# Reordering the layer norm's power, the unit maxima, the scatters and one score maximum in a sixteen-image attention pipeline

## What is computed

```python
x = x + _L0_conv_ref(_gn(x), w_qkv, pos_embedding, w_out, b_out)   # group norm, windowed attention
t = _to_tokens(x)                                                  # 16 images x 256 tokens
t = t + _L1_attn_ref(_ln_t(t), w_qkv, b_qkv, w_out, b_out)         # layer norm, full attention per image
t = t + _L1_ffn_ref(_ln_t(t), router_w, ..., fc2_b)                # layer norm, 8 experts, 2 per token
```

```python
dots = jnp.einsum('bhwid,bhwjd->bhwij', q, k) * scale
dots = dots + pos_embedding[_REL_IDX[:, :, 0], _REL_IDX[:, :, 1]]
attn = jax.nn.softmax(dots, axis=-1)
out = jnp.einsum('bhwij,bhwjd->bhwid', attn, v)
```

## Time and profile before

| | us |
|---|---|
| three runs | 706.55, 712.59, 710.5 |
| median | 710.5 |
| the profiled execution, as the device reports it | 709.77 |
| span of that execution in the profile | 708.0 |

### The profile page before, as it was taken

The page is one execution under the profiler, slowest core; times in us unless marked ns, Lnnn a source line. Parts: engine busy times, 40 slices in busy tenths (PEclk is TensorE's granted clock), DMA queues, the critical chain, the costliest instruction groups (busy, mean ns, idle before and its releaser), DMA issues.

```text
span 708.0 us, 18292 instructions
## 1 busy us (share of the span) xinstructions
PE 598.8 (85%) x6460; PEld 479.6 (68%) x6460; DVE 438.5 (62%) x1325; ACT 410.4 (58%) x915; POOL 396.2 (56%) x503
## 2 busy tenths in 40 slices
PE   4877889999989899899899998988975799999910
PEld 3656667777767777677677776766655688888810
DVE  5534666767767677677776777765433365555625
ACT  2445576787676667766767677444411366666600
POOL 5665653454546576665665765642376066666643
PEclk9799999999999999999999999999996899999975
DMA  7100220231422414224133242243841122233237
GB/s 213 25 2 1 54 54 13 50 69 56 120 43 91 118 37 119 57 86 126 42 104 89 66 122 57 85 124 91 270 182 49 47 87 87 84 91 91 72 135 254
DMA packets 54511, 63.08 MB, mean 89 GB/s; under 512 B 12978, under 2 KB 47794, under 8 KB 53906
## 3 DMA queue, kind: packets, MB, share of 16 engines
q1 hardware_dynamic: 48294, 49.59, 25.3%
q0 software_dynamic: 4544, 9.38, 3.9%
q10 hardware_dynamic: 1584, 2.95, 1.2%
HBM read 35.74 MB, written 28.64 MB: 91 GB/s over the span
## 4 chain that ended last, share of the span: by engine, by line
PE 42%; POOL 17%; issue 15%; DVE 10%; ACT 7%; DMA 6%; SPq 2%; ACTq 0%; DVEq 0%; POOLq 0%
POOL slots L549 5%; POOL pa L623 4%; POOL pa L631 3%; PE pG L1192 3%; PE pSA L1264 3%; DMA slots<-sel_dram 2%; PE pSB L1438 2%; PE pTA L1438 2%; PE pTB L1438 2%; PE pSA L1438 2%; PE pTA L1349 2%; DVE pa L994 2%; PE pOA L1449 2%; PE pOB L1449 2%; PE pOB L1293 2%
## 5 line engine op out<-in xcount | busy, mean ns | idle before, releaser
L623 POOL TENSOR_TENSOR pa<-pa,mxa 128x512 f32<-128x512 f32 x64 | 66.7, 1042 | 110.9 <-DVE mxa L1017 110.8
L664 POOL DMA_INDIRECT ysl<-yo,dst x78 | 75.5, 968 | 59.7 <-DVE yo L1154 45.3
L631 POOL TENSOR_TENSOR pa<-pa,rca 128x512 f32<-128x512 f32 x64 | 67.0, 1047 | 63.5 <-DVE rca L1037 63.3
L760 ACT ACTIVATE ptb<-pTB 128x512 f32<-128x512 f32 x128 | 76.6, 599 | 43.1 <-PE pTB L1275 42.7
L549 POOL DMA_INDIRECT slots<-rec,slot x64 | 65.1, 1017 | 15.9 <-issue 13.2
L777 ACT ACTIVATE pta<-pTA 128x512 f32<-128x512 f32 x64 | 38.5, 602 | 56.1 <-PE pTA L1349 55.6
L1027 DVE TENSOR_REDUCE sma<-pa 128x8 f32<-128x512 f32 x64 | 43.8, 684 | 37.8 <-ACT pa L754 37.8
L754 ACT ACTIVATE pa<-pa 128x512 f32<-128x512 f32 x64 | 40.2, 628 | 42.2 <-POOL pa L623 41.9
L1349 PE MATMUL pTA<-ident,pa 128*128 128x128 f32 x256 | 40.3, 281 | 24.0 <-DVE pa L994 14.7
L979 DVE TENSOR_REDUCE mxb<-pSA 128x2 f32<-128x512 f32 x64 | 44.0, 688 | 25.1 <-PE pSA L1240 24.5
L1275 PE MATMUL pTB<-q,kbd 100*128 100x256 f32 x256 | 56.1, 301 | 0.1
(11 more groups left out here) (227 smaller groups left out, 1738.3 us busy)
## 6 DMA issues: line engine op xcount, KB each, us to landing
slots<-sel_dram SPq DMA_DIRECT2D x16, 1040.0 KB
kbd<-kst SPq DMA_DIRECT2D x128, 48.0 KB, 2.2
q<-qst SPq DMA_DIRECT2D x64, 96.0 KB, 2.2
xt<-slots SPq DMA_DIRECT2D x39, 130.0 KB, 2.2
xch<-x_ch_dram SPq DMA_DIRECT2D x4, 512.0 KB, 5.8
xt<-x_tok_dram SPq DMA_DIRECT2D x16, 128.0 KB, 2.3
xch<-t SPq DMA_DIRECT2D x16, 128.0 KB, 4.6
fw<-f_dram SPq DMA_DIRECT2D x1, 2048.0 KB
```

The lines of the kernel that those rows point to most:

```text
L623: pool.tensor_tensor(pa[:, u, :, :], pa[:, u, :, :], mxa[:, u % 2, :].unsqueeze(2).to_broadcast([128, 8, WIN]), ALU.subtract).then_inc(sa_ ...
L631: pool.tensor_tensor(pa[:, u, :, :], pa[:, u, :, :], rca[:, b, :].unsqueeze(2).to_broadcast([128, 8, WIN]), ALU.mult).then_inc(sa_nrm, 1)
L664: pool.indirect_dma_start(ysl, bass.IndirectOffsetOnAxis(ap=dst[:, t % YB, n:n + 1], axis=0), yo[:, t % YB, n, :], None).then_inc(y_dma[t ...
L760: a.activation(ptb[:, h % PTBUFS, :, :], pTB[:, :].rearrange("p (a b) -> p a b", a=2), ACT.Exp).then_inc(st_exp, 1)
```

## The change

The same instructions run, with the same operands and the same waits; six blocks of code stand elsewhere. On DVE the unit maxima of u = 0 and 2 come directly behind the bias adds of steps 0 and 4, and those of u = 1 and 3 directly behind the reciprocals of steps 1 and 5, instead of at steps 2 and 6. At step 6 the score maximum comes ahead of the two remainders. On POOL the power for `tn1` goes from step 4 to step 3, behind `mine` and ahead of L631; the two scatters of step 3 go behind L631; the bias add `t1b` of step 5 goes behind L631. The lists of PE, ACT and SP are the same.

```diff
@@ POOL, iteration
-                    if n == 4 and M is not None:
-                        pool.wait_ge(m_eps, M.j + 1)
-                        pool.tensor_tensor(rs1[:, :], rs1[:, :], half[:, 0:2], ALU.pow).then_inc(m_pow, 1)
-                    if n == 5 and M is not None:
-                        pool.wait_ge(m_t, M.j + 1)
-                        wait(pool, r_t, M.j - TB + 1)
-                        pool.tensor_tensor(t1b[:, M.j % TB, :, :], t1[:, :, :], bo1s[:, :, :], ALU.add).then_inc(m_tb, 1)
...
-                    if n == 3:
-                        depart(K, n)
+                    if n == 3 and M is not None:
+                        pool.wait_ge(m_eps, M.j + 1)
+                        pool.tensor_tensor(rs1[:, :], rs1[:, :], half[:, 0:2], ALU.pow).then_inc(m_pow, 1)
...
-                    if n != 3:
-                        depart(K, n)
+                    if n == 5 and M is not None:
+                        pool.wait_ge(m_t, M.j + 1)
+                        wait(pool, r_t, M.j - TB + 1)
+                        pool.tensor_tensor(t1b[:, M.j % TB, :, :], t1[:, :, :], bo1s[:, :, :], ALU.add).then_inc(m_tb, 1)
+                    depart(K, n)
@@ DVE, iteration
-                    if M is not None and n == 6:
...
-                        v.scalar_tensor_tensor(kst1[:, 1, :], pM[:, 0:TOK], bk1s[:, 0:1], kst1[:, 0, :].bitcast(f32),
...
                         v.tensor_reduce(mxb[:, Bm.par, n % 2, n // 2 * 2:n // 2 * 2 + 2], bank[:, :].rearrange("p (a k) -> p a k", a=2), AX.X,
                                         ALU.max, negate=True).then_inc(sb_max, 1)
+                    if M is not None and n == 6:
...
+                        v.scalar_tensor_tensor(kst1[:, 1, :], pM[:, 0:TOK], bk1s[:, 0:1], kst1[:, 0, :].bitcast(f32),
...
+                    if A is not None and n % 4 == 0:
+                        u = n // 2
+                        b = u % 2
+                        v.wait_ge(sa_add, A.j * AU + (u + 1))
+                        wait(v, sa_sub, A.j * AU + (u - 1))
+                        v.tensor_reduce(mxa[:, b, :], pa[:, u, :, :], AX.X, ALU.max).then_inc(sa_max, 1)
...
-                    if A is not None and n % 2 == 0:
-                        u = n // 2
...
-                        v.tensor_reduce(mxa[:, b, :], pa[:, u, :, :], AX.X, ALU.max).then_inc(sa_max, 1)
...
                         v.reciprocal(rca[:, b, :], sma[:, b, :]).then_inc(sa_rcp, 1)
+                    if A is not None and n % 4 == 1:
+                        u = n // 2 + 1
...
+                        v.tensor_reduce(mxa[:, b, :], pa[:, u, :, :], AX.X, ALU.max).then_inc(sa_max, 1)
```

More of the change, by code:

```diff
@@ L966, in iteration @@
                                         rco[:, :, :].unsqueeze(3).to_broadcast([128, 2, H1, D1]), ALU.mult).then_inc(ot_nrm, 1)
-                    if M is not None and n == 6:
-                        v.wait_ge(m_qhi, M.j + 1)
-                        v.scalar_tensor_tensor(kst1[:, 1, :], pM[:, 0:TOK], bk1s[:, 0:1], kst1[:, 0, :].bitcast(f32),
-                                               ALU.add, ALU.subtract).then_inc(m_klo, 1)
-                        v.scalar_tensor_tensor(qst1[:, 2, :], pM[:, TOK:2 * TOK], bq1x[:, 0:1], qst1[:, 0, :].bitcast(f32),
-                                               ALU.add, ALU.subtract).then_inc(m_qlo, 1)
                     if M is not None and n == 3:
@@ L980, in iteration @@
                                         ALU.max, negate=True).then_inc(sb_max, 1)
+                    if M is not None and n == 6:
+                        v.wait_ge(m_qhi, M.j + 1)
+                        v.scalar_tensor_tensor(kst1[:, 1, :], pM[:, 0:TOK], bk1s[:, 0:1], kst1[:, 0, :].bitcast(f32),
+                                               ALU.add, ALU.subtract).then_inc(m_klo, 1)
+                        v.scalar_tensor_tensor(qst1[:, 2, :], pM[:, TOK:2 * TOK], bq1x[:, 0:1], qst1[:, 0, :].bitcast(f32),
+                                               ALU.add, ALU.subtract).then_inc(m_qlo, 1)
                     if M is not None and n == 3:
@@ L1011, in iteration @@
                         last.then_inc(r_tn, 1)
-                    if A is not None and n % 2 == 0:
-                        u = n // 2
-                        b = u % 2
-                        v.wait_ge(sa_add, A.j * AU + (u + 1))
-                        wait(v, sa_sub, A.j * AU + (u - 1))
-                        v.tensor_reduce(mxa[:, b, :], pa[:, u, :, :], AX.X, ALU.max).then_inc(sa_max, 1)
                     if M is not None and n == 5:
```

## The result

The changed kernel takes 725.4 us (median of 4 runs, 723.05 to 730.07) against 709.4 us before (4 runs, 706.55 to 712.59): a ratio of 1.0243, 95% interval 1.020 to 1.0286. The forecast was slower by 9.5 us, 720; by the ratio the loss is 17 us, which would be some 728 on the median that the forecast started from, above the 726 to which its range reached. The way was right, the size too small.

The account below looks back on a forecast made before the run. PE was taken as the bound (26.22 us busy of 28.29 an iteration). Step 4 loses 17.6 us, 6.9 and 0.6 come back, 0.2 is added: 10.3 slower on 709.8, so 720; range 702 to 726.

Parts of the forecast that it names:

- the held half at step 4: Step 4: tn1's second half, held on DVE until POOL's subtraction and the remainder behind it end; 1.35 us of PE idle.
- the early maximum of unit 1: Unit 1's maximum, moved behind the reciprocals of step 1: it stands in time in which DVE waited, at no cost.
- the sum: Whole kernel: 17.6 us lost at step 4, minus 6.9 and 0.6 given back, plus 0.2: 10.3 us slower.
- The term of step 4: Step 4: PE turns tn1 1.35 us later in the iterations of images 1 to 13, 17.6 us; bounds 0 and 1.35.
- the first rival: Step 4: DVE gets in between POOL's subtraction and remainder; PE waits 1.1 us at tn2; 5.7 slower, 715.5; chance 0.25.
- The gain: PE's waits at steps 6 and 7 shrink: 0.65 us back per iteration with scatters, 0.58 without.
- The query transfers: Next step 0: the first transfer lands about 294.2, before PE needs it; no cost if PE gains under a us.

## Why the prediction was wrong in size

Three steps failed: the held half at step 4 (1.35 us forecast, 0.85 measured); the early maximum of unit 1, put at nothing (0.45 us of waiting measured); and, by far the most, new waits of PE whose price was reckoned at nothing or at their own length, with the clock at 1.00 everywhere. In the profiled execution the iterations of images 1, 6, 7 and 9 lose 13.7 us, where the forecast's terms had 2.9; all the rest loses 6.6, where they had 7.4 (of the 10.3 us of the sum).

**Right: where and how.** The changed place that costs is step 4, by DVE's tn1 beside POOL's subtraction. The subtraction starts 0.08 us after the maximum, the first half passes, the second is held to 0.08 us behind it; the kernel with the waiting subtraction shows that the hold is the cause, and the moves of unit 2, alone and undone, that the whole loss hangs on that move (1.0288 and 1.0006). With the hold alone taken away 1.0139 is left, and 1.0030 with the products in PE's waits, so most of that rest is the clock.

**The term of step 4 was mis-sized.** "I take that as the nearest row (two full-width POOL operations back to back)": 1.35 us for tn1. It was 0.58 for tn1 and 0.27 for tn2, 0.85, the course of the first rival, which had put 1.1. DVE got in between L617 and L639. The row of L1049 was a bad guide for this pair; the run with the remainder ahead shows that it is right for another.

**The gain was right, and a loss beside it was missed.** "So an iteration with scatters gives back 0.83 + 0.27 − 0.45 = 0.65 us" came out: 0.83 gone, 0.45 at step 7. But of the maxima of units 1 and 3 the working asked only whether they "stand in time in which DVE waited". It did not ask what POOL's earlier subtraction would then stand beside. For unit 1 that is L917, 0.94 us for 0.15, and PE waits 0.45 for the places. The net of an ordinary iteration, 0.70 forecast and 0.85 measured, is near only because two errors cancel.

**The query transfers.** "If PE were a whole us earlier there, that transfer would be the next limit; at less it costs nothing." This step failed too. It was reckoned from one ordinary iteration and a median landing time of 2.2 us. In the trace of before the transfer took 3.4 us to land in the iterations of images 7 and 8, and PE waited 0.11 and 0.10 us for it: there was nothing left to gain there. In an ordinary iteration (image 12) PE came to its product 0.97 us after the landing, in the changed kernel 0.09 us after it. tn1's delay is not the reason, since it makes PE and the transfers late alike: with unit 2 put back PE waits 0.11 us there, with unit 2 alone moved it has 0.96 us left. Most of the time that was used up is, by our reading, the 0.65 us that PE gains behind the instructions that make the queries; no run takes this gain away alone. So PE now waits where the landing takes longer: 0.6 to 1.2 us in the iterations of images 6 to 8 (3.05, 3.05 and 3.67 us to land). PE's waits for these transfers over the whole execution (us, number), for the kernel before with the landing time, the changed kernel, unit 2 alone moved, and unit 2 put back:

```profile
  PE pSB L1240: 0.5, 1
DMA to landing us min/median/max: 2.2/2.2/3.4
...
  PE pSB L1243: 5.3, 6
...
  PE pSB L1246: 0.5, 1
...
  PE pSB L1249: 4.5, 7
```

These waits alone do not make the loss: the kernel with unit 2 put back has 4.5 us of them and is as fast as before. Why the landing takes longer in some iterations is open.

**The clock.** No term or rival held it, since it was 1.00 in the window that was read the earlier trace rows; each wait was priced at its own length. The iterations of images 6 to 9 take 126.5 us together, and 120.1 in the profile of the same order with the filling products, where the clock stays up; of these 6.4 us the times show 3, with intervals that overlap. With the subtraction that waits the times themselves show it, 717.4 and 710.2. So these falls hang on PE's idle time at the waits for the queries. Other falls follow other waits: those of the kernel with unit 2 alone moved, and the one of before. And a fall doesn't follow from each: behind 0.61 and 0.68 us in the iteration of image 8 the clock stayed at 1.00, and so it did in the kernel with unit 2 put back, behind 1.16 and 0.68. What decides that is open. So are the 3.0 us of the iteration of image 1, which the working had at 0.75 (1.35 less 0.6): there PE waits 1.11 us for tn1, and the clock falls from 66 us on. With the same wait it did not fall there in two other runs, the remainder first (27.35 us for this iteration) and step 6 put back (27.54, against 27.98 before), though in both the iteration ahead of it was 1.6 to 1.7 us longer. No run changed this place alone.

## What to carry to other kernels

When an order lets one of DVE and GpSimd start earlier, list what the other does in that stretch, and look for the forms that are held: here a tensor_scalar on float32, and a tensor_tensor of two elements with both inputs in SBUF, each as long as the GpSimd instruction beside it. Do it for every place where the moved instruction's successors land, not for the moved instruction's own slot. And where PE has little idle time, look for the iteration in which the next limit is worst (here the longest landing, not the median), not the ordinary one, and read the clock behind each new wait.

## What the runs showed that was not expected

DVE's held instruction ended 0.02 to 0.10 us after the POOL instruction that held it, in every such row above. Whether it is let in between two POOL instructions that follow each other without a gap depends on the pair: yes between L617 and L639, no between L615 and L621. And two waits of PE, 0.6 us for a transfer and 0.7 for a score add, could be followed by 13 us at half clock (216 to 229): that iteration was 6.3 us longer than before, several times what the rows themselves show.
